# Routing tables built later and wider, the last row scale a slot earlier, and fewer warm-up products, in an attention-and-experts kernel

## The reference

```python
x = x + _L0_xattn_ref(_layernorm(x, axis=-1), ctx_512, W_k, b_k, ln_gamma, ln_beta)
x = x + _L0_ffn_ref(_layernorm(x, axis=-1), Wg, W1, W2, W3)
# _L0_ffn_ref:
scores = jnp.einsum('btd,ed->bte', x, Wg)
topk_s, topk_i = jax.lax.top_k(scores, 2)
probs = jax.nn.softmax(topk_s, axis=-1)
for e in range(8):
    h = silu(x @ W1[e].T) * (x @ W2[e].T)          # 352 hidden
    y = y + w[..., e:e + 1] * (h @ W3[e].T)
```

## Time and profile before

| | |
|---|---|
| median of 3 runs | 388.02 us (388.01 to 388.85) |
| the profiled execution | 388.37 us, of which the span is 386.6 us |
| busy share of the span | PE 93%, DVE 71%, ACT 68%, POOL 42% |
| mean granted PE clock | 0.961 |

### The profile page before, as it was taken

One profiled execution on the slowest core, in us unless ns is written; L12 is line 12 of the kernel. 1 busy time (PEld: TensorE's weight loads), 2 busy tenths in 40 slices (PEclk: granted clock), 3 DMA queues, 4 the chain that ended last, 5 costly groups with the idle time before them and its releaser, 6 DMA issues.

```text
span 386.6 us, 8316 instructions
## 1 busy us (share of the span) xinstructions
PE 357.8 (93%) x2317; PEld 235.7 (61%) x2317; DVE 272.8 (71%) x725; ACT 263.4 (68%) x455; POOL 163.6 (42%) x200
## 2 busy tenths in 40 slices
PE   8998999978979778889999999999999999999981
PEld 7554576756946445556666666666666666666640
DVE  2367788988796999995757676666767575757660
ACT  2388999966684988976666657575666666665750
POOL 2124748557334134545253434444343435253331
PEclk9999999998559899999999999999999999999998
DMA  6999999999412133355544445353535354544524
GB/s 226 412 409 401 323 412 388 367 339 357 162 19 66 31 54 57 54 86 88 103 68 98 77 91 84 82 89 77 101 67 109 61 105 68 98 76 91 81 31 54
DMA packets 21947, 57.62 MB, mean 149 GB/s; under 512 B 4816, under 2 KB 4944, under 8 KB 20368
## 3 DMA queue, kind: packets, MB, share of 16 engines
q0 software_dynamic: 8736, 20.53, 30.0%
q1 hardware_dynamic: 12016, 30.27, 20.8%
q10 hardware_dynamic: 1152, 6.29, 4.6%
HBM read 38.17 MB, written 18.91 MB: 148 GB/s over the span
## 4 chain that ended last, share of the span: by engine, by line
PE 73%; DVE 10%; issue 5%; ACT 4%; DMA 4%; POOL 2%; POOLq 0%; ACTq 0%; DVEq 0%
PE bank L1236 34%; PE bank L1270 17%; PE bank L1094 4%; PE bank L1227 4%; PE bank L1028 3%; PE bank L1256 3%; PE bank L1136 3%; DMA stage<-in_xT 2%; DVE stage L784 2%; PE bank L1114 2%; DVE stage L786 1%; DVE Wp L812 1%; PE bank L1121 1%; DMA out<-kvj_s,sidx 1%; ACT stage L660 1%
## 5 line engine op out<-in xcount | busy, mean ns | idle before, releaser
L967 DVE SCALAR_TENSOR_TENSOR stage<-W,w3sc,stage 128x512 f16<-128x512 f16 x117 | 84.2, 748 | 6.5 <-ACT stage L660 6.5
L1270 PE MATMUL bank<-stage,n_s 128*128 128x512 f16 (+1 forms) x351 | 82.2, 379 | 1.8 <-issue 1.5
L1236 PE MATMUL bank<-Wp,kvg_s 128*128 x480 | 78.2, 313 | 3.5 <-DVE kvg_s L973 3.5
L660 ACT ACTIVATE stage<-W,w3sc 128x512 f16 x117 | 80.1, 717 | 0.0
L1236 PE MATMUL bank<-Wp,kv_s 128*128 x456 | 75.9, 317 | 4.2 <-DVE kv_s L973 4.2
L506 POOL DMA_INDIRECT out<-oT_s,sidx x20 | 34.1, 1706 | 75.4 <-ACT oT_s L687 68.3
L1236 PEld LDWEIGHTS bank<-Wp,kvg_s 128*128 128x128 f16 x480 | 46.7, 98 | 29.6 <-issue 5.1
L1236 PEld LDWEIGHTS bank<-Wp,kv_s 128*128 128x128 f16 x456 | 44.9, 99 | 29.8 <-issue 5.5
L991 DVE TENSOR_TENSOR n_s<-bank,n_s 128x384 f16<-128x384 f32 x39 | 21.7, 557 | 55.1 <-ACT n_s L673 55.1
L506 POOL DMA_INDIRECT out<-kvj_s,sidx x19 | 32.4, 1707 | 65.7 <-ACT kvj_s L687 63.1
L1270 PEld LDWEIGHTS bank<-stage,n_s 128*128 128x128 f16 (+1 forms) x351 | 34.2, 98 | 35.1 <-issue 2.3
(11 more groups left out here) (184 smaller groups left out, 554.5 us busy)
## 6 DMA issues: line engine op xcount, KB each, us to landing
Wp<-in_w SPq DMA_DIRECT2D x8, 1408.0 KB, 10.8
W<-in_w ACTq DMA_DIRECT2D x8, 768.0 KB, 7.7
stage<-in_xT SPq DMA_DIRECT2D x4, 1024.0 KB, 9.8
W<-in_x SPq DMA_DIRECT2D x12, 256.0 KB, 10.9
out<-W SPq DMA_DIRECT2D x12, 256.0 KB, 8.7
n_table<-n_s SPq DMA_DIRECT2D x8, 256.0 KB, 7.2
n_table<-x_s SPq DMA_DIRECT2D x8, 256.0 KB, 5.5
stage<-in_x SPq DMA_DIRECT2D x4, 256.0 KB, 9.4
```

The source lines that it names most:

```text
L660: eng.activation(w3p[t % 2][:, c * D:(c + 1) * D], W3[:, bass.ds(e * W3N + c * D, D)], ACT.Copy, scale=w3sc[:, bass.ds(e, 1)]).then_inc(s_ ...
L967: eng.scalar_tensor_tensor(w3p[r][:, W3N + c * D:W3N + (c + 1) * D], W3[:, bass.ds(e * W3N + c * D, D)], w3sc[:, bass.ds(e, 1)], w3p[r][:, ...
L1236: mm = eng.matmul(bank[2 * which + r][:, 0:H], n_, w_, start=(c == 0 and k == 0), stop=(c == DC - 1 and k == 2))
L1270: mm = eng.matmul(ybank(t - 1)[:, :], h_, w_, start=(c == 0 and k == 0), stop=(c == HC - 1 and k == 2))
```

## The change

Seven edits that belong together:

1. `scale_in(15)` is issued in slot 14, after `residual(12)`, instead of first in slot 15.
2. `columns(0)` moves from slot 14 to slot 16, between `residual(14)` and `chosen(10)`; `places(1)` from slot 15 to slot 17; `columns(1)` from slot 16 to behind the last slot.
3. For the first three groups (`WIDE = 3`) `columns` is two DVE compares of 8 x 128 elements each (`oh_r` and `oh_c`), with `ramp` repeated for each column and `rf16` or `qf16` (new f16 tiles) repeated along 128. `tok1` is no longer multiplied in there: ACT does it in place by the new `number(q)`, four activations of 128x256 a group.
4. PE's `table(0)` moves from slot 15 to behind `router(13)`, `table(1)` to ahead of `router(15)`, `table(2)` to behind `counts`.
5. `weight_sums` goes a slot later, `weight_root` to POOL's slot 17, `weight_scale` behind `chosen(12)`.
6. ACT's `w3_square(0)` goes a slot later, and `w3_square(1)` from slot 15 into the closing work; both `w12_high(0, ·)` follow it.
7. `WARM_LAST` (slots 14 and 15) goes from 12 to 8, `WARM_GATHER` from 36 to 24.

```diff
-WARM_GATHER = 36
+WARM_GATHER = 24
...
-WARM_LAST = 12
+WARM_LAST = 8
...
+WIDE = 3
...
+            def number(q):
+                eng.wait_ge(s_ohp, q + 1)
+                for i in range(TPB):
+                    cols = slice(i * TOPK, (i + 1) * TOPK)
+                    eng.activation(oh_r[:, q % 2, cols, :], oh_r[:, q % 2, cols, :], ACT.Copy,
+                                   scale=tok1[:, q * TPB + i:q * TPB + i + 1]).then_inc(s_ohn, 1)
...
             def columns(q):
...
+                if q < WIDE:
+                    cols, ring, shape = slice(g0 * TOPK, (g0 + m) * TOPK), slice(i0, i0 + m * TOPK), [P, m * TOPK, P]
+                    eng.tensor_tensor(oh_r[:, a, ring, :], ramp[:, 0:1, :].to_broadcast(shape),
+                                      rf16[:, cols, None].to_broadcast(shape), ALU.is_equal).then_inc(s_ohp, 1)
+                    eng.tensor_tensor(oh_c[:, a, ring, :], ramp[:, 0:1, :].to_broadcast(shape),
+                                      qf16[:, cols, None].to_broadcast(shape), ALU.is_equal).then_inc(s_ohc, 1)
+                    return
...
             def slot(s):
-                if row(s):
+                if row(s) and s < G - 1:
                     scale_in(s)
...
+                if s == G - 2:
+                    scale_in(G - 1)
+                if s == 16:
+                    columns(0)
+                if s == 17:
+                    places(1)
...
-                if s == 14:
-                    columns(0)
-                if s == 15:
-                    places(1)
-                if s == 16:
-                    weight_scale()
-                    columns(1)
...
+            columns(1)
             chosen(G - 4)
+            weight_scale()
             places(2)
```

More of the change, by code:

```diff
@@ L194, in build @@
         rf = sb("rf", [P, G * TOPK])
+        rf16 = sb("rf16", [P, G * TOPK], F16)
+        qf16 = sb("qf16", [P, G * TOPK], F16)
         ramp = sb("ramp", [P, 3, P], F16)
@@ L254, in build @@
         s_r = sem("s_r")
-        s_oh, s_cs, s_rank, s_cntp, s_pick, s_pos, s_rq, s_rqf, s_ohr, s_ohc, s_tab, s_sel, s_tabT, s_gp, s_et, s_eoff, s_esp, s_jcol = [
-            sem(n) for n in ("s_oh", "s_cs", "s_rank", "s_cntp", "s_pick", "s_pos", "s_rq", "s_rqf", "s_ohr", "s_ohc", "s_tab",
+        s_oh, s_cs, s_rank, s_cntp, s_pick, s_pos, s_rq, s_rqf, s_ohp, s_ohn, s_ohr, s_ohc, s_tab, s_sel, s_tabT, s_gp, s_et, s_eoff, s_esp, s_jcol = [
+            sem(n) for n in ("s_oh", "s_cs", "s_rank", "s_cntp", "s_pick", "s_pos", "s_rq", "s_rqf", "s_ohp", "s_ohn", "s_ohr", "s_ohc", "s_tab",
                              "s_sel", "s_tabT", "s_gp", "s_et", "s_eoff", "s_esp", "s_jcol")]
@@ L586, in slot @@
                     o_evac(b)
-                if s in (14, 15):
-                    w3_square(s - 14)
+                if s == 15:
+                    w3_square(0)
+                if s == 16:
+                    number(0)
             def w3_square(k):
@@ L640, in _ @@
             router_exp(0)
+            number(1)
             turned(G - 1)
+            number(2)
+            w3_square(1)
             w12_high(0, 0)
+            w12_high(0, 1)
             w3_square(2)
-            w12_high(0, 1)
             w3_square(3)
@@ L771, in places @@
                 eng.wait_ge(s_rq, 2 * q + 1)
-                eng.tensor_copy(rf[:, cols], ri[:, cols]).then_inc(s_rqf, 1)
+                eng.tensor_copy((rf16 if q < WIDE else rf)[:, cols], ri[:, cols]).then_inc(s_rqf, 1)
                 eng.wait_ge(s_rq, 2 * q + 2)
-                eng.tensor_copy(qf[:, cols], qi[:, cols]).then_inc(s_rqf, 1)
+                eng.tensor_copy((qf16 if q < WIDE else qf)[:, cols], qi[:, cols]).then_inc(s_rqf, 1)
             def columns(q):
@@ L1063, in table @@
                 i0, a = g0 % TPB * TOPK, g0 // TPB % 2
+                if q < WIDE:
+                    eng.wait_ge(s_ohn, g0 + m)
+                    eng.wait_ge(s_ohc, q + 1)
                 for c in range(m * TOPK):
-                    eng.wait_ge(s_ohr, g0 * TOPK + c + 1)
-                    eng.wait_ge(s_ohc, g0 * TOPK + c + 1)
+                    if q >= WIDE:
+                        n = (g0 - GROUPS[WIDE][0]) * TOPK + c + 1
+                        eng.wait_ge(s_ohr, n)
+                        eng.wait_ge(s_ohc, WIDE + n)
                     mm = eng.matmul(bank[5][:, 0:P], oh_c[:, a, i0 + c, :], oh_r[:, a, i0 + c, :], start=(q == 0 and c == 0),
@@ L1180, in slot @@
                     weight_norms()
-                if s == 15:
-                    table(0)
             eng.wait_ge(s_const, 1)
@@ L1204, in _ @@
             router(G - 3)
+            table(0)
             turn_n(G - 1)
             router(G - 2)
+            rank(3)
             table(1)
-            rank(3)
             router(G - 1)
-            table(2)
             rank(4)
             counts()
+            table(2)
             table(3)
```

## The result

The changed kernel takes 391.48 us (median of 19 runs, 389.31 to 393.78), the one before 388.02 us (19 runs, 386.04 to 390.4). The ratio is 1.0079, 95% interval 1.0052 to 1.0105: slower by 0.8%, where 0.6% faster was forecast and the range ended at 388.0.

A forecast was written before the change was run, and what follows sets the result against it. It took DVE's weight splitting from w3_scale on as fixed, and ACT's closing queue as the new bound ahead of it. A 2.3 us gain gave 388.37 - 2.3 = 386.1, against the median 388.02 - 2.3 = 385.7; range 383.0 to 388.0.

The forecast's parts named there:

- The frame: From w3_scale's start (123.94 us before) all that follows moves with it; the 3.3 us from w3_sums stay.
- The rows: In the row slots, the last residual is done at 88.5 us where it was 94.2, 5.7 us earlier.
- The wide compare: On DVE, 1024 elements take 1.28 us, or 0.65 at the double rate; a table costs 2.4 or 1.3.
- ACT's closing queue becomes the bound: After the row slots, ACT's queue, 13.8 us before, gains number(2) (1.5 us) and one w3_square (1.5).
- The gain is 101.2 - S: Gain at w3_sums, 120.64 before, now 19.4 us after number(2) starts; 2.3 us for a start at 98.9.
- S: Time at which number(2) starts ACT's closing queue; forecast 98.9 us.
- The 19.4 us from S to `w3_sums`: Closing work from number(2)'s start: ACT's queue gives 19.3 us, the way through the gather 18.5 to 19.6.
- quicker rival: PE's clock stays up or compares run at double rate: gain 3.3 to 5.2 us, 382.8 to 384.7; chance 0.28.
- WARM_GATHER costs nothing: Before the gathered rows land, 24 products take 5.1 us at the lower clock, longer than the landing needs.
- S = 98.9: number(2) starts at 98.9 us, behind the first compare of columns(2), with PE's clock falling around 89.6.
- ahead of its reader: weight_root at POOL's slot 17 is done at about 93 us, before its reader needs it.
- The slower rival: Too few warm products: clock falls at 83 us, before router(10), number(2) starts at 101.4; together 389.5 us, chance 0.11.

The follow-up runs named there:

- c4: The changed kernel with all tables by narrow pairs (no number()) and w3_square(1) moved between turned(13) and turned(14) on ACT; ratio 0.9996 to the kernel before.
- e3: The changed kernel once more, nothing edited, one execution for a second profile; 391.81 us.
- a3: The changed kernel with w3_square(1) moved out of ACT's closing queue to between turned(13) and turned(14); ratio 0.9991 to the kernel before.
- e2: The changed kernel with only ACT's order mended: w3_square(1) and (2) in idle stretches, router_exp(1) right behind both splits; ratio 0.9928 to the kernel before.
- d1: The changed kernel with WIDE = 2: third table by narrow pairs, no number(2) in ACT's closing queue; ratio 0.9970 to the kernel before.
- a1: The changed kernel with WARM_GATHER back at 36, nothing else; ratio 1.0034 to the kernel before.
- b1: The kernel before with WARM_GATHER 24 and WARM_LAST 8, nothing else; ratio 1.0013 to the kernel before.
- e1: The changed kernel with only warm products mended: WARM_GATHER 36, WARM_LAST 12, six more ahead of router(11); ratio 1.0019 to the kernel before.
- a4: The changed kernel with WIDE = 0: all tables by narrow pairs in the new places, no number() on ACT; ratio 0.9978 to the kernel before.

## Why the prediction was wrong, point by point

- **The frame** (what counts is the start of `w3_scale`; POOL's root behind `w3_sums` is fixed): right. What follows the start is within 0.4 us of before's 262.7 in all kernels but c4 (0.9), and `w3_sums` to `w3_scale` is 3.3 us in all.
- **The rows**: right, a little too large. Last row forecast 5.7 us earlier, measured 4.9 (its `residual` starts at 88.47 for 93.37). The 0.8 us are `residual(14)`, which is done at 85.3 and not at 84.5, since `norm(12)` ends at 84.4 for 83.8. In e3, with its late load, the last `residual` is only 3.3 us earlier (90.08).
- **The wide compare**: right. 1.28 us forecast, 1.21 to 1.24 measured, the end without the double rate (0.65). The Trainium skill's rule ("Vector Engine (DVE) Microarchitecture Reference", section 5.1) holds in this trace.
- **"ACT's closing queue becomes the bound"**: the mechanism was right. The gather waited for the store of `wrow` and not for `gidx`, as forecast, and a3 and e2 show that a shorter queue brings it forward and the time down. d1 brings the time down too, but in its profile not by an earlier gather.
- **"The gain is 101.2 - S"** is the step that failed. S itself was 99.59 and 101.40 in two executions, for 98.9 forecast. The 19.4 us from S to `w3_sums` were 22.05 and 22.02. Of the 2.65 us, 0.4 are the exponential, at S + 9.1 for 8.7 (`number(2)` 1.61 us for 1.5, the `w3_square` with the reading of its sum 1.65 for 1.5, the rest 5.86 for 5.66). 0.7 are the store, whose way from the weights to the gather was 3.0 us for 2.3: the sum took the shorter of two landing times, 2.2, and 0.1 for all else. And 1.6 us come after PE's transposes, 3.48 us to `w3_sums` for the 1.9 taken from before, since PE was at the lower clock when the rows landed. There `w3_sums` waited last, 1.04 us, for something that the prediction does not have: PE's sum over `w3sq`, which stands behind ten warm products. With 22.05 in the formula the balance is 98.6 - S, a loss at the S that was forecast, and a gain only for the quicker rival's.
- **"WARM_GATHER costs nothing"** is the term behind that 1.6 us. I set 24 products against the landing as if the gather started right behind `gidx`, although the same prediction lets it wait for the store, which here was 4 us later. With PE idle for 4.45 us the clock fell. a1 puts the cost of the cut at 1.7 us here, with a wide interval, and b1 finds none that shows where the gather is not held. 0.9 us of PE's wait come from the gather itself, 2.17 us on POOL for 1.25. It is 2.1 to 2.2 us in a1, e1 and e3 too, where POOL also stood 2.9 to 3.0 us for the store, and 1.24 to 1.26 in all other profiles, also in d1 and a3, where the store held it as well. Why is open.
- **"S = 98.9"** was 0.7 and 2.5 us too early. In e3, near the median, the 5.7 us between 386.1 and 391.81 are 2.5 of S, 2.6 from S to `w3_sums`, and 0.6 in the rest. Of the 2.5, 1.6 are the late load, of which the prediction, made from one execution, could know nothing: so that part of the miss is chance. How many executions have that load late, and whether the changed kernel's have it more often than before's, two profiles can't say; e1 and e2, each measured beside the kernel before, show that most of the loss doesn't hang on it. The forecast also has the clock at 0.50 from 89.6 up to S; it fell at 89 and was back at 92.4 in the first profile, fell at 91 and was back at 98 in e3. That S was 99.59 in the first profile although the clock was back is the next point.
- **`weight_root` "ahead of its reader"**: wrong. DVE waits 1.84 us for it at 95.91, and from there to the compare that `number(2)` waits for it has no gap. `rank(2)`, which it needs next, was through at 95.0, so S would have been some 1.2 us earlier without this wait (an estimate from these times, not tried); in e3 `rank(2)` was through only at 98.1, as was `weight_scale`, and the wait cost nothing. POOL's `norm` took 2.30 us beside the wide compares, for 1.13. That the compares stretch it is what a4 and c4 show: with narrow tables in the same places it took 0.85 and 0.94 us there, 0.91 and 0.81 beside the second table for 2.32, and DVE did not wait for the root.
- **The slower rival** had the outcome and part of the reasons: ACT's longer queue costing more than the rows gave, and the lower clock after 24 products. Its S of 101.4 was met by e3 (101.40), but by luck: its cause, the clock falling already before `router(10)`, was not seen in either profile. It priced the lower clock in the first groups of 12 products, where the first took 2.74 us for 1.96 and nothing of it showed behind `w3_scale`; the price was paid in the ten warm products ahead of them. Its own terms (0.2 lost and some 2 us) add up to 390.2 and not to 389.5. At 0.11 it had too little: the break-even S had an error of its own, which I gave no chance.

## What to carry to other kernels

When work is moved off one engine, add up the queue that receives it, from its last point of synchronisation to everything that reads from it, stores and round trips too, and compare with the room that this queue had before. Here 1.7 + 1.5 us on ACT ahead of one tiny exponential kept the gather where it was, although DVE had its list ready 3.5 us earlier; the same operations in ACT's idle stretches, with the exponential ahead of what nobody waits for, made the change a gain of 0.7%. And size warm-up products by the wait that they are to bridge in the new schedule, not in the old. And take a second profile of the same kernel before a term is sized to half a microsecond: here two executions of one program differed by 1.8 us ahead of the closing work.

## What was not expected of the hardware

- POOL's 128x512 `tensor_scalar` took 2.30 and 2.32 us while DVE ran the 128x1024 two-source compares, against 0.77 to 1.29 us for the other fourteen in the same kernel, and 0.81 to 0.94 us in the same two places in a4 and c4, where DVE ran narrow one-source compares.
- An 8 KB store from the end of the operation that makes its data to the start of the operation that waits for it: 3.0 us in both profiles of the changed kernel, 2.9 in a1 and e1, but 4.6 in d1.
- The same gather instruction took POOL 1.24 to 1.26 us in thirteen profiles and 2.14 to 2.24 in four.
- A load of W1 and W2 that lands up to 1.9 us too late at 66 us in some executions of one program, and not in others.
- Activations of 128x256 f16 from SBUF to SBUF in place cost 0.42 us each (four in 1.69 to 1.71).
